# Two cross-attentions in a fused decoder kernel: exponentials times values on column strips of TensorE, and a tile that is normalised once instead of twice

## The reference, cut to what matters

```python
def _L0_xattn_ref(q, k, v):          # KVH = 8, G = 4, D = 8
    qh = q.reshape(b, s, KVH, G, D).transpose(0, 2, 3, 1, 4)
    kh = k.reshape(b, s, KVH, D).transpose(0, 2, 1, 3)
    vh = v.reshape(b, s, KVH, D).transpose(0, 2, 1, 3)
    scores = jnp.einsum('bkgsd,bktd->bkgst', qh, kh) * scale
    attn = jax.nn.softmax(scores, axis=-1) / DROPOUT
    out = jnp.einsum('bkgst,bktd->bkgsd', attn, vh)
    return out.transpose(0, 3, 1, 2, 4).reshape(b, s, E)
...
x = x + jnp.tanh(g_xattn[0]) * _L0_xattn_ref(_layernorm(x, axis=-1), ctx_512, ctx_512)
...
x = x + jnp.tanh(g_xattn[1]) * _L1_xattn_ref(_layernorm(x, axis=-1), ctx_512, ctx_512, L1_xattn_Wc, L1_xattn_bc)
```

## Time and profile before

| | |
|---|---|
| median of 3 runs | 1719.53 us |
| lowest and highest | 1709.69 and 1721.87 us |
| span of the profiled execution | 1714.7 us |
| its mean TensorE clock, as a share of 2.4 GHz | 0.803 |
| PE, PEld, DVE, ACT, POOL busy | 1178.8, 778.6, 1084.7, 783.1, 883.5 us |
| 16 DMA engines | 144 GB/s in the mean |

### The profile page before, as it was taken

How to read it: one execution, slowest core, us unless ns; L and a number is a source line. 1 busy time by engine, 2 the same in 40 slices (tenths; PEclk the granted TensorE clock), 3 DMA queues, 4 the chain that set the end, 5 groups by cost and what they waited for, 6 DMA issues and landing times.

```text
span 1714.7 us, 32329 instructions
## 1 busy us (share of the span) xinstructions
PE 1178.8 (69%) x9122; PEld 778.6 (45%) x9132; DVE 1084.7 (63%) x2699; ACT 783.1 (46%) x1599; POOL 883.5 (52%) x846
## 2 busy tenths in 40 slices
PE   4999998133333299999678777871676777846775
PEld 2566665112221266666555555650454444532243
DVE  5899996666666466666444454442765555747898
ACT  3566665122222166666445454441343333433574
POOL 2343343266666633333377777715888888516100
PEclk9999999555555599999777887785788888878878
DMA  9555554032323599999899999984344434100011
GB/s 209 161 151 154 148 154 135 15 115 104 111 106 110 154 281 308 310 301 304 206 242 237 252 246 248 247 199 101 53 54 55 55 55 55 28 1 1 13 37 49
DMA packets 283470, 247.09 MB, mean 144 GB/s; under 512 B 117584, under 2 KB 270032, under 8 KB 282960
## 3 DMA queue, kind: packets, MB, share of 16 engines
q1 hardware_dynamic: 234192, 169.99, 38.9%
q0 software_dynamic: 49152, 75.53, 20.8%
HBM read 111.93 MB, written 117.77 MB: 134 GB/s over the span
## 4 chain that ended last, share of the span: by engine, by line
DMA 24%; DVE 20%; PE 18%; POOL 16%; issue 13%; SPq 4%; ACT 3%; DVEq 1%; POOLq 0%; ACTq 0%
DMA xs<-V 13%; POOL x L632 11%; DMA arena<-xs 8%; PE bank L1493 4%; DVE arena L1318 3%; DMA xs<-arena,V 2%; PE bank L1369 2%; POOL rs L575 2%; PE bank L1381 2%; DVE arena L971 2%; PE bank L1355 2%; PE bank L1569 2%; PE bank L1370 2%; SPq L518 2%; DVE arena L1316 2%
## 5 line engine op out<-in xcount | busy, mean ns | idle before, releaser
L632 POOL DMA_INDIRECT x<-ys,idx x256 | 404.1, 1578 | 129.2 <-issue 57.6
L650 POOL DMA_INDIRECT xs<-V x192 | 187.1, 974 | 207.7 <-DMA xs<-V 188.5
L1493 PE MATMUL bank<-arena,region 128*128 128x128 f16 x2496 | 253.2, 245 | 1.6 <-ACT arena L834 0.9
L834 ACT COPY arena<-bank 128x640 f16<-128x640 f16 x192 | 132.3, 689 | 190.2 <-PE bank L1569 188.2
L1569 PE MATMUL bank<-arena 128*128 128x128 f16 x1440 | 145.2, 240 | 105.3 <-DMA arena<-xs 101.5
L1381 PE MATMUL bank<-arena 128*72 128x256 f32 (+1 forms) x768 | 212.0, 417 | 0.1
L1493 PEld LDWEIGHTS bank<-arena,region 128*128 (+1 forms) x2496 | 187.0, 111 | 19.2 <-issue 6.2
L1569 PEld LDWEIGHTS bank<-arena 128*128 128x128 f16 x1440 | 97.0, 107 | 113.3 <-DMA arena<-xs 85.4
L573 POOL TENSOR_TENSOR ve<-mv,epsilon 128x1 f32<-128x1 f32 x96 | 39.5, 412 | 202.0 <-DVE mv L912 180.0
L1381 PEld LDWEIGHTS bank<-arena 128*72 128x72 f32 (+1 forms) x768 | 117.2, 158 | 46.4 <-issue 13.5
L982 DVE TENSOR_REDUCE arena<-bank 128x8 f32<-128x512 f32 x192 | 124.1, 675 | 15.5 <-PE bank L1355 14.3
(11 more groups left out here) (204 smaller groups left out, 2557.6 us busy)
## 6 DMA issues: line engine op xcount, KB each, us to landing
ys<-arena SPq DMA_DIRECT2D x96, 512.0 KB
arena<-xs SPq DMA_DIRECT2D x288, 160.0 KB
xs<-idx SPq DMA_DIRECT2D x52, 256.0 KB, 2.4
arena<-in_wpairs SPq DMA_DIRECT2D x32, 256.0 KB, 2.6
arena<-in_wpairs SPq DMA_DIRECT2D x128, 64.0 KB, 2.5
x<-ys,idx POOLq DMA_INDIRECT x256, 6.3
out<-arena SPq DMA_DIRECT2D x16, 256.0 KB, 2.2
xs<-idx SPq DMA_DIRECT2D x52, 64.0 KB, 2.1
```

Source lines behind the costliest of these rows:

```text
L632: pool.indirect_dma_start(tile_x(t), None, ys[t // HT], bass.IndirectOffsetOnAxis(ap=idx[:, t, k:k + 1], axis=0), compute_op=ALU.add).then ...
L650: pool.indirect_dma_start(xs[t // HT], bass.IndirectOffsetOnAxis(ap=at_row[:, t, n % 8:n % 8 + 1], axis=0), ROW[t % NROW], None).then_inc( ...
L834: act.copy(XTP[g % 2][q], tpm[n % 2]).then_inc(R_["xt"], 1)
L1493: mm = pe.matmul(o, lhs(a, w, k), rhs(a, w, k), start=(n == 0), stop=(n == 3 * KT - 1))
```

## The change

The values get strips. `VD` now holds for a pair only the pair's own columns: 128 columns are divided among the key heads, 16 (32) each, of which the first `d` are the head's values and the next is one. A pair thus has 32 (64) columns, and its product goes to its own 32 (64) partitions of `bank[6]` on its own column strip of the array, without adding up. `bank[6]` is then filled in 128 partitions, and its copy and its turning back (L749, L1405) take 128 rows instead of 72 or 68. The sums stand behind each head's columns, where the reciprocals and the last product (L993, L1001) now read them.

The tile is normalised once: `XG` has one copy, and DVE writes it with one instruction instead of two. In its place PE turns each `g` twice, with two plain matmuls against the identity onto the two halves of the partitions, instead of one transpose of both.

```diff
     W0 = C + 8
-    XG = [carve([G, C + W0]) for _ in range(2)]
+    XG = [carve([G, W0]) for _ in range(2)]
...
-    VD = [carve([2, 4 * W0]) for _ in range(2)]
+    VD = [carve([2, P]) for _ in range(2)]
...
                 def blocks(v, half):
 
-                    at = v[half * S:(half + 1) * S, 0, half * d:(half + 1) * d]
-                    return bass.AP(at.tensor, at.offset, [list(at.ap[0]), [4 * W0, 2], [w + 2 * d, npair], [1, d]])
+                    return v[half * S:(half + 1) * S].rearrange("p b (n h w) -> p b n h w", h=2, w=P // nk)[:, :, :, half, 0:d]
...
-                        act.copy(PVS[0:w].rearrange("p g (b s) -> p g b s", b=2),
-                                 bank[6][0:w, :].rearrange("p (b g s) -> p g b s", b=2, g=G)).then_inc(a["pvs_ready"], 1)
+                        act.copy(PVS.rearrange("p g (b s) -> p g b s", b=2),
+                                 bank[6][:, :].rearrange("p (b g s) -> p g b s", b=2, g=G)).then_inc(a["pvs_ready"], 1)
...
-                for d in dst[:-1]:
-                    dve.tensor_scalar(d, src, mv[:, j, 0:1], rs[:, j, :], ALU.subtract, ALU.mult)
-                dve.tensor_scalar(dst[-1], src, mv[:, j, 0:1], rs[:, j, :], ALU.subtract, ALU.mult).then_inc(l["out"], 1)
+                dve.tensor_scalar(dst, src, mv[:, j, 0:1], rs[:, j, :], ALU.subtract, ALU.mult).then_inc(l["out"], 1)
...
-                        o = bank[7][:, 0:G * w].rearrange("p (g w) -> p g w", g=G)
+                        o = bank[7].rearrange("p (g k w) -> p g k w", g=G, k=nk)
                         dve.wait_ge(a["ot_ready"], t)
-                        dve.reciprocal(RC[:, :, 0:nk], o[:, :, C:w]).then_inc(a["rc_done"], 1)
+                        dve.reciprocal(RC[:, :, 0:nk], o[:, :, :, d]).then_inc(a["rc_done"], 1)
...
+                    cg = P // npair
                     for p in range(npair):
                         e = EX[(b * nsc + p // 2 + (0 if nsc == 2 else 2 * j)) % 4]
-                        mm = pe.matmul(bank[6][0:w, b * 256:(b + 1) * 256], VD[j][:, b, p * w:(p + 1) * w],
-                                       e[:, (p % 2) * 256:(p % 2 + 1) * 256], start=(p == 0), stop=(p == npair - 1))
+                        mm = pe.matmul(bank[6][p * cg:(p + 1) * cg, b * 256:(b + 1) * 256], VD[j][:, b, p * cg:(p + 1) * cg],
+                                       e[:, (p % 2) * 256:(p % 2 + 1) * 256], start=True, stop=True)
...
                         for g in range(G):
-                            mm = pe.transpose(bank[7][:, g * w:(g + 1) * w],
-                                              PVS[0:w, g, :], ident[0:w, 0:w])
+                            mm = pe.transpose(bank[7][:, g * P:(g + 1) * P], PVS[:, g, :], ident)
...
                         for g in range(G):
-                            mm = pe.transpose(bank[0][:, g * P:(g + 1) * P],
-                                              XG[j][:, g, 0:2 * C], ident)
+                            for half in range(2):
+                                mm = pe.matmul(bank[0][half * C:(half + 1) * C, g * P:(g + 1) * P], XG[j][:, g, 0:C], ident, start=True, stop=True)
```

More of the change, by code:

```diff
@@ L60, in const_columns @@
     at, out = 0, {}
-    for name, width in (("ident", P), ("ones0", 4 * 8), ("ones1", 2 * 4)):
+    for name, width in (("ident", P), ("ones0", 8), ("ones1", 4)):
         out[name] = (at, width)
@@ L77, in attention_table @@
     for layer, (nk, d) in enumerate(LAYERS):
-        pair = np.arange(nk // 2)[None, :, None]
-        head = 2 * pair + (r[:, :, None] >= S)
-        put(f"ones{layer}", np.arange(nk)[None, None, :] == head)
+        put(f"ones{layer}", np.arange(nk)[None, :] % 2 == (r >= S))
     return t
@@ L590, in attention @@
                     for b in range(2):
-                        pool.tensor_copy(VD[j][:, b, 0:npair * w].rearrange("p (n w) -> p n w", w=w)[:, :, C:w],
-                                         ones.rearrange("p (n k) -> p n k", k=nk)).then_inc(a["vd_set"], 1)
+                        pool.tensor_copy(VD[j][:, b, :].rearrange("p (k w) -> p k w", k=nk)[:, :, d], ones).then_inc(a["vd_set"], 1)
                 def step(t, j):
@@ L981, in maxima @@
                     dve.wait_ge(a["mx_ready"], n)
-                    dve.tensor_reduce(XG[j][:, u * gpu:(u + 1) * gpu, 2 * C:C + w],
+                    dve.tensor_reduce(XG[j][:, u * gpu:(u + 1) * gpu, C:w],
                                       bank[2 + u % 2][:, :].rearrange("p (g k t) -> p g k t", g=gpu, t=S),
@@ L1000, in step @@
                             dve.wait_ge(a["ont_ready"], t - 2)
-                        dve.tensor_tensor(heads(ON[1 - j]), o[:, :, 0:C].rearrange("p g (k d) -> p g k d", d=d),
+                        dve.tensor_tensor(heads(ON[1 - j]), o[:, :, :, 0:d],
                                           RC[:, :, 0:nk].unsqueeze(3).to_broadcast([P, G, nk, d]), ALU.mult).then_inc(a["on_ready"], 1)
@@ L1033, in step @@
                             dve.wait_ge(F["tp_ready"], t - 3)
-                        norm(t - 2, 2 + j, 3, [XD[j]], tile_x(t - 2))
+                        norm(t - 2, 2 + j, 3, XD[j], tile_x(t - 2))
                     if inside(t + 3):
@@ L1037, in step @@
                             dve.wait_ge(a["t2_ready"], t + 2)
-                        norm(t + 3, 1 - j, ln, [XG[1 - j][:, :, r * C:(r + 1) * C].rearrange("p g (k d) -> p g k d", d=d) for r in range(2)],
-                             heads(tile_x(t + 3)))
+                        norm(t + 3, 1 - j, ln, XG[1 - j][:, :, 0:C].rearrange("p g (k d) -> p g k d", d=d), heads(tile_x(t + 3)))
                     if layer == 1 and inside(t - 2):
@@ L1434, in step @@
                         for g in range(G):
-                            mm = pe.transpose(bank[1][0:w, g * P:(g + 1) * P], XG[1 - j][:, g, C:C + w], ident)
+                            mm = pe.transpose(bank[1][0:w, g * P:(g + 1) * P], XG[1 - j][:, g, 0:w], ident)
                         mm.then_inc(a["t2_ready"], 1)
```

## The result

The changed kernel takes 1730.92 us in the median of four runs (1725.76 to 1735.3), beside 1716.62 us for the kernel before in four runs. The measured ratio is 1.0118, 95% interval 1.0084 to 1.0151; the two medians alone, 14.3 us apart, would make it 1.0083. **It is slower by 1.2%** by the measured ratio; 1715.3 us and no change within 1% were forecast. The time lies in the range of 1702 to 1738 us, but on the side of rival B. The profiled span is 1733.5 us, 18.8 more than before.

The account below looks back on a forecast made before the run. DVE was taken to bound 4.68 us and PE 3.3 us of the first attention's 8.14 us period. Terms -2.8 - 2.4 + 0.5 + 0.5 = -4.2 gave span 1710.5, plus 4.8 makes 1715.3 us; range 1702 to 1738.

Parts of the forecast that it names:

- rival B: First attention: more PE idle time lowers the clock, slowing PE's 3.3 us of the chain; 14 us, 1729 us; chance 0.09.
- five steps of 0.216 us: First attention's value products on four strips: eight records overlap only partly, 1.08 us instead of 1.73, twice a tile.
- the lower bound: First attention's value products: all four calls run together, 0.43 us; forecast would fall another 7 us, to 1708.
- DVE bounds 4.68 us of the period: First attention: DVE bounds 4.68 us, PE 3.3 us of 8.14; shortening PE's block beside DVE doesn't shorten the period.
- A changed array: PE changing between strips and the full array costs 0.10 us; two more changes a tile, +0.20.
- L1405 with 128 rows: Turning back the result, on the chain: 0 to +0.18 us a tile, taken as +0.02, +0.5 us over 23 tiles.
- DVE's second normalisation: One 0.40 us instruction a tile goes; worth nothing in the first attention, where the remaining one still takes about 1.16 us.
- The second attention's body: From 1201 to 1472 us the chain is POOL's 113 gathers; its length stays as before.
- The first tiles: First four tiles of the first attention: PE's block on the chain falls from 4.5 to 3.87 us, -2.8 us in all.
- The last tiles of the first attention: Products in a row save 1.4 us, the tile before 1.0, L1405 gives back 0.2; together put at -2.4 us.
- The tail of the second: Second attention from 1472 us: three tiles +0.33 each, more at half clock, DVE -0.4; together +0.5 us.
- The 4.8 us from span to time: Whole kernel: median of three runs 1719.5 minus profiled span 1714.7, added to the forecast span 1710.5.

Follow-up runs that it names:

- other sequence: Kernel before, with the products of exponentials and values of each tile's second sequence left out in the first attention's loop: 1725.58 us against 1708.97, ratio 1.009.
- values three times: Changed kernel with every matmul of exponentials and values done three times in the first attention's loop: 1706.25 us against 1710.15, ratio 0.9976.
- spread: Changed kernel with two more waits on PE before the value products in the first attention's loop, no work added: 1703.65 us against 1708.97, ratio 0.9971.
- one sequence: Kernel before, with the products of exponentials and values of each tile's first sequence left out in the first attention's loop: 1709.82 us against 1710.15, ratio 0.9995.
- turning alone: Kernel before with only the single normalisation and the eight plain turning matmuls on two strips, values as before: 1715.59 us against 1710.15, ratio 1.0042.
- two filled kernels: Changed kernel with every value matmul done three times or twice in the first attention's loop: 1706.25 us (ratio 0.9976) and 1703.8 us (ratio 0.9968).

## Why the prediction was wrong

**The step that failed is the size of the products on strips**: "record two must follow record one on its own strip, and only then may the next call's first start", five steps of 0.216 us. The eight records span 0.64 us with the last one's own 0.38, so the starts lie within 0.26, in two groups of four: as I read it, all four first records run together, then all four second ones (the records don't say which call they belong to). That makes two steps where I had five. It is the lower bound that I had named, 0.43 us and some, and I had set it aside for a rule of order that no row showed. The Trainium skill's page TensorEngine Tiling (Array Packing), section Overview, gives up to four times the speed for strips of at most 32 columns. The trace agrees with that table (1.89 against 0.64 us, and 1.73 against 0.48 without the last record's tail, 3.6 times). The 16 records of the turning came out the same way, at their lower bound: 1.04 - 0.27 = 0.77 us for seven steps of 0.11, so eight steps and not nine, 0.87 us for 0.97.

**What hung on it** was the idle time. I put it at 0.7 us and gave rival B, the falling clock, 9%, because PE "would stay near 92%" busy. It was 2.06 us: two products 0.60 us shorter each and the turning 0.10 make up 1.30 of the difference. With 0.33 or 1.20 us of idle time in one piece the runs keep the clock at 1.00, so with the size that I had assumed it would have been kept, as far as these runs tell, and the time would have been about theirs, 0.2 to 0.3% below the kernel before. Rival B named the right mechanism and place, PE's own part of the chain at half the clock. Its price was 14 us for the whole, from half the clock in a fifth of the time and 0.6 us a tile; the clock of 0.87 means about a quarter, the loop lost 0.98 us a tile, 23.6 in all, of which the ends gave 7.2 back. That its 1729 us stand so near to the measured 1730.92 is luck. That the clock falls without strips for these products (other sequence left out) and stays with them (values three times, spread) shows that it is PE's idle time, and the pairs of runs with equal matmuls (one sequence and other sequence, changed and spread) show that it is how this idle time lies.

Point by point, for the rest:

- *DVE bounds 4.68 us of the period, PE the rest, and a faster block on PE shortens nothing:* right. At full clock the period is 8.15 to 8.16 us in every version but the one with the turning alone.
- *A changed array costs 0.10 us:* the products' first start is still that much behind the turning (222.32 after eight steps of 0.109 from 221.35), right.
- *L1405 with 128 rows costs 0 to 0.18 us on the chain, taken as 0.02:* right; tiles at full clock have the old period.
- *DVE's second normalisation is worth nothing in the first attention, and the one left takes 1.16 us beside POOL:* right, 1.16 us at 226.07.
- *The second attention's body is POOL's and doesn't move:* right; 113 gathers in a stretch of 272 us, from 1218 us on, as in the earlier trace rows; the row of POOL's groups by line:

```profile
L629 POOL DMA_INDIRECT x<-ys,idx x113 | 180.8, 1600 | 31.1 <-issue 31.1
```

- *The first tiles, -2.8 us:* 5.0 measured. The block is some 1.3 us shorter than I had it, by the same sizes as above. The chain of the changed kernel no longer passes through it there, but for instance through a load of expert weights:

```profile
43.13 5.76 DMA arena<-in_wpairs
...
48.91 0.02 ACT region L725
```

- *The last tiles of the first attention, -2.4:* 2.2 measured, but that is partly luck. The terms of the sum (-1.4, -1.0, +0.2) make -2.2, not -2.4; and PE runs part of this stretch at half the clock in the changed kernel (scores of 0.21 us each at 294 us). In the two filled kernels, whose code there is the same, the last four tiles took 25.2 us, no less than before.
- *The tail of the second, +0.5:* the second attention as a whole gave back 0.3, too little to split.
- *The 4.8 us from span to time:* a run's time stands 1.8 us above its span (1735.3 and 1733.5), so 3 of the 4.8 were a difference between runs; with the fourth run the kernel before came to 1716.62 and not 1719.5. That shifts the forecast by 3 us and decides nothing.

Not settled: the exact condition under which the clock falls. One piece of 1.20 us leaves it alone, one of 1.89 us doesn't, and neither do 0.79 and 1.20 us that lie 0.6 apart, so the longest piece is not the whole of it. Why the records of four fp32 calls start in groups of four was not tried either.

## What to carry to other kernels

Work taken off an engine that is not the bound leaves idle time; on TensorE that can cost the clock, and with it the part of the chain where TensorE is the bound. Before making a hidden block of matmuls shorter, work out how much idle time will be left and how it lies, pieces that are close together included. Where the profile then shows a lower clock, spread the same calls over the time that another engine needs: two waits turned 1.2% slower into 0.3% faster here. And where a row's nearest relative shows that a resource works in parallel, take the bound with full overlap as a case of its own and ask what the rest of the kernel would do then.

## What the runs showed of the hardware

- fp32 calls on four strips of 32 columns run four at a time: eight records of 256 columns in 0.64 us, against 1.89 us on the full array; on two strips of 64, 16 records of 128 columns in 1.04 us.
- With the same matmuls (idle times of a tile at full clock, period 8.15 us), the changed kernel's clock was 1.00 with the idle time in three pieces (0.72, 0.58, 0.62 us), and 0.87 with one piece of 2.06 us or two of 0.79 and 1.20 us close together. The kernel before without the products of one sequence had 1.00 with two pieces 2.4 us apart (0.58, 1.10) and 0.90 with one of 1.89 us.
- More work can be faster: 16 more calls a tile made the changed kernel 1.4% faster.
